# Attention: two PSUM banks for the scores and four for the products behind the maxima, where each had three

## The reference

```python
x = x + xattn(layernorm(x), ctx, ctx, Wq, Wk, Wv, bv, Wo, bo)
x = x + ffn(layernorm(x), controller, f1, bias, f2)
# xattn: 16 heads of 32 features
scores = einsum('bhsd,bhtd->bhst', qh, kh) / sqrt(32)
scores = where(triu(ones) without element [0, 0], -inf, scores)   # a token sees earlier tokens only
probs  = softmax(scores, axis=-1)
out    = einsum('bhst,bhtd->bhsd', probs, vh) ... @ Wo.T + bo
# ffn: 128 experts each pick one token of every group of 32, two small layers with relu, sum back
```

## Time and profile before

| | us |
|---|---|
| median of three runs | 1225.07 |
| the profiled execution, its own time | 1224.32 |
| its span, first to last instruction | 1222.6 |
| PE busy in the span | 1145.3 (94%) |
| DVE busy | 860.9 (70%) |
| ACT busy | 599.5 (49%) |
| POOL busy | 536.2 (44%) |
| exponentials (L1072), 608 of them | 304.7 |
| products for maxima (L1159), 768 | 278.2 |
| score products (L1180), 768 | 260.0 |

### The profile page before, as it was taken

One profiled execution on the slowest core, in us unless ns is written; L12 is line 12 of the kernel. 1 busy time (PEld: TensorE's weight loads), 2 busy tenths in 40 slices (PEclk: granted clock), 3 DMA queues, 4 the chain that ended last, 5 costly groups with the idle time before them and its releaser, 6 DMA issues. The chain is left out here.

```text
span 1222.6 us, 28711 instructions
## 1 busy us (share of the span) xinstructions
PE 1145.3 (94%) x11328; PEld 788.3 (64%) x11328; DVE 860.9 (70%) x2200; ACT 599.5 (49%) x1110; POOL 536.2 (44%) x740
## 2 busy tenths in 40 slices
PE   7999999999999999999999999998899997879886
PEld 6787888886555555555555555553578886767664
DVE  7765677763777777777777777774478886755765
ACT  4222222214565566556556655656244443437774
POOL 1000000012777666777766677777566640001344
PEclk9999999999999999999999999999989998989998
DMA  8978877885566444556644456622588874863555
GB/s 288 349 257 295 275 270 262 291 254 157 131 138 139 102 101 105 118 132 139 139 100 103 101 117 136 139 73 69 211 295 265 261 254 125 297 230 87 166 167 166
DMA packets 169733, 223.42 MB, mean 183 GB/s; under 512 B 9728, under 2 KB 97280, under 8 KB 168576
## 3 DMA queue, kind: packets, MB, share of 16 engines
q1 hardware_dynamic: 169600, 221.61, 61.6%
HBM read 143.69 MB, written 77.63 MB: 181 GB/s over the span
## 5 line engine op out<-in xcount | busy, mean ns | idle before, releaser
L1072 ACT ACTIVATE p_t<-p_bank 128x512 f32<-128x512 f32 (+1 forms) x608 | 304.7, 578 | 185.0 <-PE p_bank L1180 182.1
L936 DVE CUSTOM_DVE_ANT_0 tried<-p_bank,ban 128x128 bf16<-128x128 f32 (+3 forms) x512 | 237.2, 485 | 69.9 <-PE p_bank L1159 66.7
L1159 PE MATMUL p_bank<-k_stack,q_stack 96*128 96x512 f32 (+3 forms) x768 | 278.2, 377 | 4.9 <-DVE mx_ab L939 0.8
L1180 PE MATMUL p_bank<-q_stack,k_stack 97*128 97x512 f32 (+3 forms) x768 | 260.0, 359 | 11.2 <-ACT p_t L1072 9.8
L939 DVE TENSOR_REDUCE mx_ab<-p_bank 128x1 f32<-128x512 f32 x256 | 176.1, 688 | 57.2 <-PE p_bank L1159 55.6
L1159 PEld LDWEIGHTS p_bank<-k_stack,q_stack 96*128 96x128 f32 x768 | 144.3, 189 | 103.0 <-issue 39.8
L1180 PEld LDWEIGHTS p_bank<-q_stack,k_stack 97*128 97x128 f32 x768 | 145.6, 191 | 46.4 <-ACT p_t L1072 29.9
L821 POOL TENSOR_SCALAR_AFFINE_SELECT p_t<-p_t 128x128 f32<-128x128 f32 (+2 forms) x288 | 103.7, 362 | 160.2 <-ACT p_t L1072 153.5
L1199 PE MATMUL p_bank<-p_t,v_tile 128*32 128x512 f32 (+3 forms) x1536 | 164.7, 497 | 0.0
L832 POOL TENSOR_TENSOR p_sum<-p_sum,p_t 128x512 f32<-128x512 f32 x128 | 160.1, 1287 | 0.0
L1448 POOL TENSOR_TENSOR kept_o_sum<-kept_o_sum,kept_x_in 128x512 f32<-128x512 f32 x32 | 40.9, 1281 | 179.1 <-ACT kept_o_sum L1476 178.4
(11 more groups left out here) (132 smaller groups left out, 2079.3 us busy)
## 6 DMA issues: line engine op xcount, KB each, us to landing
q_stack<-q_hi SPq DMA_DIRECT2D x64, 256.0 KB, 6.8
k_stack<-k_hi SPq DMA_DIRECT2D x30, 512.0 KB, 9.6
kept_f<-in_f SPq DMA_DIRECT2D x5, 2048.0 KB, 10.7
x_in<-in_x SPq DMA_DIRECT2D x8, 1024.0 KB, 9.9
x_t<-in_x_t SPq DMA_DIRECT2D x8, 1024.0 KB, 9.0
k_hi<-k_hi_s SPq DMA_DIRECT2D x8, 1024.0 KB, 5.9
k_lo<-k_lo_s SPq DMA_DIRECT2D x8, 1024.0 KB, 7.8
v_rows<-v_out SPq DMA_DIRECT2D x8, 1024.0 KB, 7.7
```

Source lines behind the costliest of these rows:

```text
L936: dve.tensor_tensor_reduce(scrap, got, ban0[:] if i == 0 else ban[:, CH - w:CH], 1.0, -3e38, ALU.add, ALU.max, to[:, col:col + 1]).then_in ...
L1072: act.activation(pt[:, k % SLOTS_P, u * m:(u + 1) * m, 0:w], bank[:, SB + n % SR, 0:m * w].rearrange("p (m w) -> p m w", m=m), ACT.Exp, sc ...
L1159: pe.matmul(bank[:, to, 0:w], qs[it % SLOTS][0:R, i * P // CH, h, i * P % CH:i * P % CH + P], ks[it % SLOTS][0:R, h, t0:t0 + w], start=Tru ...
L1180: mm = pe.matmul(bank[:, SB + n % SR, h % m * w:(h % m + 1) * w], ks[slot][0:R + 1, h, j * P:(j + 1) * P], qs[slot][0:R + 1, sh, h, CH - w ...
```

## The change

The ring of scores gets banks 0 and 1, the ring of the products for maxima banks 2 to 5. Everything else, the order of the instructions on each engine too, stays. SR and SB appear in score() and exponential(), MR and MX in place(), and reuse() takes from it which earlier product or turn has to be read first.

```diff
         bank = ctx.enter_context(nc.psum_tensor("p2_bank", [P, 8, 512], F32))
-        SR, MR = 3, 3
-        SB, MX, OB, DB = 0, 3, 6, 7
+        SR, MR = 2, 4
+        SB, MX, OB, DB = 0, 2, 6, 7
         VB, FB, KB = 0, 2, 4
```

## The result

The changed kernel takes 1266.46 us (median of four runs, 1262.62 to 1276.84), against 1224.32 us before (four runs). The ratio is 1.036, with a 95% interval of 1.031 to 1.041: slower by 3.6%. The forecast was 1264.5 us.

A forecast was written before the change was run, and what follows sets the result against it. The tensor engine, held by PSUM bank waits, sets attention's pace. Stretches sum to 2.74 us, taken as 2.65; fifteen iterations give 39.8, first -1, last +1.5: about +40 on 1224.3, stated as 1264.5 us, range 1248 to 1277.

The forecast's parts named there:

- The round of a bank: Score bank's exponential, release, score product and next start: 1.20 us, so two banks give 0.60 per unit against ScalarE's 0.49.
- F1: Attention stretch of eight 512-wide units: last score product waits for exponential 5, values start 0.96 us later.
- F2: Attention stretch of four 384-wide and four 512-wide units, ScalarE late: third score product already waits, +0.95 us.
- F3: Attention stretch of two units of two 256-wide heads, then four of 512: last product waits for fourth exponential, +0.48 us.
- F5: Attention stretch of four 512-wide units and one of four heads: fifth unit 0.72 late, 0.27 credited, +0.45 us.
- F4: Attention stretch of one four-head unit, then four of 512: some 0.3 us VectorE wait saved, gain eaten, net nothing.
- F0: Attention stretch of five narrow maxima products, a turn and six units: 0 from the score ring, -0.1 us for VectorE waits.
- The ends of attention: First attention iteration: -1 us, partly beside the wait for placed rows; last iteration: +1.5 us, bounds 0 and 3.
- (d): Rival: tensor engine idles more in attention and its clock is lowered, some 110 us more, 1370 us; 3 in 100.
- (a): Rival: four maxima banks win, two score banks cost little if a round is under 0.98 us; 1200 us, 4 in 100.
- (b): Rival: loss and gain cancel, the kernel's time stays within 0.2% (2.5 us); 2 in 100.
- (c): Rival: loss only in F1 and F2, ring of four saves its full 1.6 us per iteration; 1241 us, 6 in 100.

The follow-up runs named there:

- e1: Kernel before with two score banks and three maxima banks, bank 2 unused: 1274.14 us, 1.040 times the kernel before.
- e3: Kernel before, still three and three banks, with sums written over the output's bank and ScalarE's output copy waiting for them: 1223.94 us, 1.000 times before.
- e2: Kernel before with three score and four maxima banks, sums written over the output's bank, output copy waiting for them: 1205.34 us, 0.983 times before.
- e6: Changed kernel (two score, four maxima banks) with exponentials over half the columns from the second iteration on: 1222.95 us, 1.000 times the kernel before.
- e7: Kernel before with one score bank and five maxima banks: 1795.44 us.
- e8: Kernel before with four score banks and two maxima banks: 1334.84 us, 1.092 times the kernel before.

## Why the prediction was right

**The round of a bank.** Forecast 1.20 us; in F1 the pairs follow at 1.20, 1.18 and 1.19, and with one bank the units at 1.19. Halving the exponential moved the round to 0.97 and cut the loss in F1 and F2 from 0.91 and 0.92 to 0.33 and 0.56; e1 shows it without the fourth maxima bank. This step is shown.

**Stretch by stretch.** F1 +0.96 forecast, +0.91 measured; F2 +0.95, +0.92; F3 +0.48, +0.39; F5 +0.45, +0.34; F4 0, -0.04; F0 "0 and -0.1", -0.06. Sum 2.74, of which I took 2.65, and 2.46 measured. The overestimate lies mostly in F3 and F5. In both I let the last product wait with its load in the open and then added 0.45 or what stood behind it before; that a maxima product fills part of such a wait is the slack that I had named and credited with 0.09. e1 shows what the fourth maxima bank took off against it: 0.6 of the 0.7 credited, but not where I had it: 0.38 in F4 (0.3 credited), 0.15 in F0 (0.1) and 0.04 in F5 (0.27). So in F5 two terms were too large and partly cancelled: the delay was 0.38 (e1), not 0.72, and the credit 0.04.

**The ends of attention.** These were mis-sized, and made good for the smaller stretches. From the start of values to the start of values, the first iteration is 3.5 us longer (43.3 against 39.8), where I had 2.65 less 1. The less 1 didn't come: the wait for the placed rows is 1.54 us in both kernels. And 0.9 is the clock, the stretch of values behind F1 at a granted 0.63 in place of 0.86.

The last iteration is 4.0 us longer (35.4 against 31.4), where I had 1.5 with an upper bound of 3. F1 and F2 wait for banks (+1.25 and +1.08), F3 is 0.31 shorter, F4 0.25 longer. But the clock seems to have a larger part in it than the ring: the stretches of values behind F0 and F1 took 3.90 and 3.31 us in place of 2.29. The kernel before had a dip of its own, behind F3:

```profile
872.57:876.47 3.90, 3.90 (x34) 1.37 (x33) 0.76 (x2) 0.81 (x2) 0.85 (x3) 0.58 0.81 249
881.29:884.60 3.31, 3.31 (x34) 1.14 (x33) 0.00 (x0) 0.99 (x3) 0.00 (x0) 0.68 0.21 79
```

```profile
832.38:834.67 2.29, 2.29 (x33) 0.90 (x32) 1.28 (x3) 0.84 (x2) 1.32 (x5) 1.00 0.50 143
850.89:855.32 4.43, 4.43 (x26) 1.00 (x25) 0.00 (x0) 0.70 (x2) 4.43 (x4) 0.50 0.16 59
```

That dip of 2.1 us seems to have cost nothing: e3, which had a granted 1.00 throughout, took 31.5 us for the same iteration, and the weight loads of its last values and sums waited 5.1 us for GpSimd in place of 1.4. With two score banks and only one slow stretch of values (3.38 us), e1 took 33.9. Without the excess of these stretches, 2.6 and 1.1 us, the changed kernel and e1 would both take 32.8, if nothing else waited in its place: as an estimate, the ring costs 1.3 us over e3's 31.5, near my 1.5, and the clock the rest. No run here separates the two fully.

One iteration late in attention is 4.0 us longer in place of 2.5, by a dip of the clock, and the one behind it 3.1, since the kernel before gained 0.6 there. Behind attention 2.8 us were gained, with the same work; from 36 us behind it to the end the granted clock was 0.97 against 0.95. Attention grew by 44.2 us (570.7 to 614.9), the span by 41.4, the forecast was 40. That these are so close is partly luck: the stretches gave less than forecast, the clock in attention took more, which I had at nothing outside rival (d), and behind attention something came back that I hadn't counted.

**The trade on the counts.** The sums of load idle looked like a gain (19.0 us to lose, 43.6 to win). e2 against e3 shows the gain that could really be had, 18.6 us; e1 against before the loss, 50 us. Of the 43.6 us, 10.1 were no bank wait, and much of the rest is hidden under the product before.

**The rivals.** (a) would need a round under 0.98, and e6 has 0.97: there the two splits take the same time per iteration, and the gain of 1.6 that (a) promised doesn't come, since F1 and F2 still lose 0.89 together. The shorter exponentials changed ScalarE's pace as well, so e6 gives the round at which the two splits are even and doesn't test the 0.98. (b) and (c) didn't come. The price of (c) doesn't follow from its own words: the full 1.6 off the 1.91 leaves 0.3 per iteration, 1229 us, where it takes off 0.8 and says 1241; either is far from 1266. (d) showed in one regular iteration of the changed kernel and in the first and the last one, and in full in e7.

## What to carry to other kernels

Price a ring of buffers by the time of one round (the consumer from start to end, its signal, the producer's load and product) over the number of buffers, and compare it with the pace of both engines; the consumer's pace alone is too short by what its instructions overlap. A sum of idle time doesn't tell which of two rings is short: read in the timeline, stretch by stretch, which wait ends last. And where two rings take turns in being short, one ring in the order of issue can beat the fixed splits: here it beat all four that were run, and gave 1.1% where moving one bank cost 3.6% and moving it the other way 9.2%.

## What the runs showed that I had not expected

The clock. The kernel before had a granted clock of 1.00 all through its regular iterations, and dips only in the first and the last one. The changed kernel, with the tensor engine waiting more, had one dip in its regular iterations:

```profile
800.00:805.00 5.00, 4.93 (x44) 2.45 (x43) 2.55 (x8) 3.00 (x7) 1.51 (x2) 1.00 0.14 52
805.00:810.00 5.00, 4.20 (x15) 2.07 (x19) 4.05 (x11) 4.26 (x9) 3.07 (x6) 0.83 0.72 175
810.00:815.00 5.00, 5.00 (x34) 2.16 (x27) 2.62 (x9) 0.95 (x3) 3.29 (x4) 0.83 1.04 218
```

The stretch F2 of that iteration lies in it (5.50 us in place of 5.09) and the values behind it (3.87 in place of 2.71), and the iteration took 39.7 us in place of 38.2. e1 has two such iterations, with the dip in the same place (40.4 us in place of 38.8, with a granted 0.73 from 425 to 430 us), e8 a mean of 0.97, e7 of 0.70. So in these kernels waits can cost more than their own length: with one score bank the rounds at full clock account for some 21 us more per iteration (57 expected against 35.7), and 15 more came with the lower clock. Why one iteration of the changed kernel dipped and its neighbours, with the same pattern, didn't, no run here shows.
